# Constant rows of the stacked queries and keys: two batches in turn instead of four

## What is computed

```
# attention of layer 0, 16 heads of 8, S = 512
scores = (q @ k.T + c2p + p2c) / sqrt(8 * 3)
# c2p[i, j] = q[i] . pos_k[bucket(i - j) + 32], p2c[i, j] = k[j] . pos_k[32 - bucket(j - i)]
out = layernorm(softmax(scores) @ v @ Wo + bo + x)
# switch feed-forward, E = 8, F = 512
e = argmax(softmax(t @ switch_w + switch_b))
y = (gelu(t @ w1[e] + b1[e]) @ w2[e] + b2[e]) * max(route_prob)
```

## Time and profile before

| what | value |
|---|---|
| time of three runs | 761.99, 763.94, 764.26 us; median 763.94 us |
| span of the profiled execution (the page gives its span only, not the execution's whole time) | 759.0 us |
| busy share PE / DVE / ACT / POOL | 77% / 69% / 58% / 28% |
| moved by DMA | 130.80 MB, mean 172 GB/s |
| mean granted TensorE clock | 0.895 of full speed |

### The profile page before, as it was taken

How to read it: one execution, slowest core, us unless ns; L and a number is a source line. 1 busy time by engine, 2 the same in 40 slices (tenths; PEclk the granted TensorE clock), 3 DMA queues, 4 the chain that set the end, 5 groups by cost and what they waited for, 6 DMA issues and landing times. The chain is left out here.

```text
span 759.0 us, 16760 instructions
## 1 busy us (share of the span) xinstructions
PE 583.0 (77%) x5262; PEld 405.4 (53%) x5262; DVE 523.5 (69%) x1838; ACT 441.8 (58%) x960; POOL 209.7 (28%) x264
## 2 busy tenths in 40 slices
PE   4359967557999999999999999551997673578880
PEld 3258853234566565666666666441986342246550
DVE  7513235726778777899999997674224799867797
ACT  3225424336788788888888887560553443376723
POOL 1714424200950391059040000025344200211200
PEclk9999987877999999999999999755999697799885
DMA  9948834999999999999984540833553100000001
GB/s 245 258 149 292 260 104 129 282 320 324 267 363 325 233 278 332 313 223 273 323 242 114 137 110 2 252 74 108 175 188 108 30 1 0 0 1 1 0 1 56
DMA packets 130450, 130.80 MB, mean 172 GB/s; under 512 B 27148, under 2 KB 106876, under 8 KB 129468
## 3 DMA queue, kind: packets, MB, share of 16 engines
q1 hardware_dynamic: 121628, 101.88, 48.6%
q0 software_dynamic: 4032, 25.73, 9.1%
q10 hardware_dynamic: 4704, 2.11, 1.2%
HBM read 73.43 MB, written 52.92 MB: 166 GB/s over the span
## 5 line engine op out<-in xcount | busy, mean ns | idle before, releaser
L1526 DVE CUSTOM_DVE_ANT_0 l0am_prob<-l0am_ps_s,l0am_bias 128x512 f32<-128x512 f32 x256 | 161.6, 687 | 48.3 <-PE l0am_ps_s L1603 38.4
L1447 ACT ACTIVATE l0am_prob<-l0am_prob,l0am_neg_top 128x512 f32<-128x512 f32 x256 | 172.0, 729 | 11.9 <-DVE l0am_neg_top L1526 11.9
L1615 PE MATMUL l0am_ps_t<-c_ident,l0am_prob 128*128 128x128 f32 x1024 | 137.8, 278 | 0.0
L1615 PEld LDWEIGHTS l0am_ps_t<-c_ident,l0am_prob 128*128 128x128 f32 x1024 | 113.4, 142 | 16.8 <-issue 15.9
L613 ACT ACTIVATE l0f_h<-l0f_psU,l0f_experts 128x128 f32<-128x128 f32 x184 | 52.4, 368 | 84.2 <-PE l0f_psU L907 84.2
L1441 ACT COPY l0am_probT<-l0am_ps_t 128x512 f32<-128x512 f32 x128 | 69.0, 589 | 45.8 <-PE l0am_ps_t L1615 45.8
L1603 PE MATMUL l0am_ps_s<-l0am_ks,l0am_qs 32*128 32x512 f32 x512 | 73.9, 647 | 14.3 <-DVE l0am_neg_top L1526 11.1
L1513 DVE COPY l0am_probT<-l0am_ps_t 128x512 f32<-128x512 f32 x128 | 81.9, 681 | 2.3 <-PE l0am_ps_t L1615 2.1
L785 DVE COPY l0f_xsT<-l0f_psT 128x128 f32<-128x128 f32 x46 | 13.4, 291 | 90.9 <-PE l0f_psT L897 90.9
L1628 PE MATMUL l0am_ps_c<-l0am_probT,l0am_v 128*9 128x128 f32 x2048 | 67.9, 273 | 0.9 <-issue 0.9
L524 POOL DMA_INDIRECT token_results<-l0f_ys,l0f_token_i x46 | 44.2, 960 | 80.2 <-DVE l0f_ys L795 79.6
(11 more groups left out here) (319 smaller groups left out, 962.1 us busy)
## 6 DMA issues: line engine op xcount, KB each, us to landing
l0am_bias<-near_terms SPq DMA_DIRECT2D x128, 192.0 KB, 5.5
near_terms<-l0am_near POOLq DMA_DIRECT2D x6, 3072.0 KB, 13.0
l0f_mine<-l0f_experts SPq DMA_DIRECT2D x46, 256.0 KB, 2.6
near_terms<-l0am_near SPq DMA_DIRECT2D x2, 3072.0 KB, 10.9
l0am_rows_k<-position_k SPq DMA_DIRECT2D x12, 448.0 KB, 8.4
position_q<-l0am_rows SPq DMA_DIRECT2D x20, 224.0 KB, 5.3
position_k<-l0am_rows SPq DMA_DIRECT2D x20, 224.0 KB, 4.9
l0f_experts<-in_L_ffn_w SPq DMA_DIRECT2D x2, 2048.0 KB, 8.4
```

What stands on the lines that cost most here:

```text
L1447: nc.scalar.activation(prob[:, k, :], prob[:, k, :], ACT.Exp, bias=neg_top[:, k:k + 1], scale=-1.0)\
L1526: dve.tensor_tensor_reduce(out=prob[:, k, :], in0=ps_s[:, j, :], in1=bias[:, j, at:at + S], scale=-1.0, scalar=HUGE, op0=ALU.add, op1=ALU.min,
L1615: last = pe.transpose(ps_t[:, u % 2, i, :], prob[:, u % SLOTS_, i * P:(i + 1) * P], ident[:, :])
```

## The change

The stacks hold two batches (`STACKS = 2`); batch b uses place b % 2. So constant rows are stored for two batches only, four DMAs instead of eight. None is issued ahead of the slots; the four follow the loads of slots 2, 5, 8 and 11. Since batches 2 and 3 overwrite the places of batches 0 and 1, SP waits, ahead of the store of their q and k chunks, until the tiles of the last group of the batch b - 2 are loaded.

```diff
+STACKS = 2
...
-        "stack": [dram(f"stacked_{n}", (MARGIN + B * HEADS * 32 * FAR_PITCH,)) for n in "qk"],
+        "stack": [dram(f"stacked_{n}", (MARGIN + STACKS * HEADS * 32 * FAR_PITCH,)) for n in "qk"],
...
-        EARLY_BLOCKS, LATE_BLOCKS = 2, tuple(range(2, 20, 3))
+        LATE_BLOCKS = tuple(range(2, 2 + 3 * 2 * STACKS, 3))
...
                     aside.load(sp)
-                    for n in range(EARLY_BLOCKS):
-                        aside.store_blocks(sp, n)
...
                     if aside and s in LATE_BLOCKS:
-                        aside.store_blocks(sp, EARLY_BLOCKS + LATE_BLOCKS.index(s))
+                        aside.store_blocks(sp, LATE_BLOCKS.index(s))
...
-    BLOCK_STORES = 2 * B + 2
+    BLOCK_STORES = 2 * STACKS + 2
...
# store_chunk
-                        dst = bass.AP(dram["stack"][side].tensor, MARGIN + b * HEADS * 32 * FAR_PITCH,
+                        if b >= STACKS:
+                            last_group = GROUPS * (b - STACKS + 1) - 1
+                            sp.wait_ge(tiles_in[last_group % 2], 32 * (last_group // 2 + 1))
+                        dst = bass.AP(dram["stack"][side].tensor, MARGIN + b % STACKS * HEADS * 32 * FAR_PITCH,
...
# store_far
-                    dst = bass.AP(dram["stack"][side].tensor, MARGIN + (b * HEADS * 32 + first) * FAR_PITCH + col,
+                    dst = bass.AP(dram["stack"][side].tensor, MARGIN + (b % STACKS * HEADS * 32 + first) * FAR_PITCH + col,
...
# load_tiles
-                        src = bass.AP(dram["stack"][side].tensor, MARGIN + n * GROUP * 32 * FAR_PITCH, [(FAR_PITCH, P), (1, S)])
+                        src = bass.AP(dram["stack"][side].tensor, MARGIN + n % (STACKS * GROUPS) * GROUP * 32 * FAR_PITCH, [(FAR_PITCH, P), (1, S)])
```

## The result

The changed kernel takes 758.27 us, median of 11 runs (755.17 to 760.38). The kernel before, run again beside it, comes to 761.47 us over 11 runs (758.77 to 764.26), the three shown ahead among them. The ratio, with its 95% interval behind it, is 0.9943 [0.9925, 0.9961]: 4.3 us faster, between 3.0 and 5.7. The two medians lie 3.2 us apart; the interval holds both values. The gain is real and not far from the 5.5 us forecast, yet both of its terms were too big. So I read the profile by stretches.

The account below looks back on a forecast made before the run. Bound taken: chains through DMA at the router's end (POOL's issues, DMA, SP, PE) and at the last slots' token loads. Gains 3.0 + 2.5 = 5.5 us from 763.94 gave 758.4 us; range 755.8 to 761.6.

Parts of the forecast that it names:

- first term: Router's end: without the two early stores, SP's first load of tokens follows POOL's last scatter sooner, gaining 3.0 us.
- B: Rival, chance 0.10: no gain at the router's end, blank rows, scatters and loads of `mine` alone make the queue; 761.4 us.
- C: Rival, chance 0.11: no gain in the last slots, SP's pace sets them or the tail takes it back; 760.9 us.
- the second call is the nearest row: Step at the router's end: same POOL, ACT and SP instructions, so its 2.05 us distance was taken, gaining 3.0 us.
- small pieces: DMA at 35 to 41.5 us, first call: blank rows, scatters and loads of `mine`, engines busy at 209 GB/s.
- rule of turns packet by packet: Router's end: DMA engines alternate between queues per packet, so the last scatter wouldn't pay for the stores; gain near 0.
- second term: Last slots: without the stores behind slots 14 and 17, slots 18 to 22 take 8.24 us, not 10.78; gain 2.5.
- if the last tokens still take over 4: End of the slots: prediction wrong if last tokens are turned over 4 us after their load's issue; 4.90 before.
- SP's wait under 1 us: Attention, q chunk of batch 3: SP's added wait for group 7's tiles holds 0.6 us, covered by 3.9 us slack.
- rival D: Chance 0.06: slower, SP's wait for group 7's tiles at batch 3's q chunk delays bias loads; +4.1, 768.0 us.
- the same 644.2 us within 1: From the attention's first operation to the span's end: time unchanged; a deviation beyond 1 us makes the prediction wrong.
- as it is: Whole program: the runs' median is 4.94 us above the profiled span, taken as time around it and left unchanged.

Follow-up runs that it names:

- Each half alone: Changed kernel with the two late stores put back (only early ones gone): 0.996; with the two early stores put back (only late ones gone): 0.9964.

## Why the prediction was right, and where its terms were not

All profiles by what their layout has in common (us):

| what | with the stores | without | difference | forecast |
|---|---|---|---|---|
| end of last scatter to first load of tokens | 5.05, 5.53, 4.30, 5.12; mean 5.00 | 3.57, 3.39, 3.38, 3.41; mean 3.44 | 1.6 | 3.0 |
| turn of slot 18 to turn of slot 22 | 10.78, 9.89, 10.29, 9.75, 9.02; mean 9.95 | 8.79, 8.47, 8.09, 7.83, 8.13, 8.09; mean 8.23 | 1.7 | 2.5 |
| start of the attention (before; changed) | 114.81, 115.97, 114.21; mean 115.0 | 111.66, 111.47; mean 111.6 | 3.4 | 5.5 |

**The direction and both mechanisms were right.** Each half alone is still faster than before, with intervals that leave out 1, and each distance follows the stores ahead of it and no others. So the first term isn't absent, as B had it, nor the second, as C had it. (Left out of the first row are the kernels whose blank rows or loads of `mine` were moved; out of the second, the two whose slot loop holds no stores at all.)

**The first term was mis-sized, 1.6 us for 3.0.** The step that failed is "the second call is the nearest row, being the same instructions of POOL, ACT and SP". The instructions are the same, but not how the blank rows lie against the scatters: ACT issues its last transfer 1.7 us after POOL's last scatter in the changed kernel's first call (39.30 and 37.65), and 2.7 us after it in the second call of before (527.6 and 524.87). That this is the reason isn't shown, but with the last three held back the distance is 1.70, 1.82 and 2.02 us, so the missing 1.4 us were there to be had, by another edit; moving the loads of `mine` gave 0.9 of them in one profile. What I costed at nothing ("small pieces" at 35 to 41.5) was a third of the wait. Nor was the second call a fixed value: its distance is 1.81 to 2.82 us over nine profiles. Rival B had pointed at just these transfers; it went wrong in giving them all of it. Its rule of turns packet by packet would have made this term near 0; the distances decide against that, 5.00 with the stores and 3.44 without.

**The second term was mis-sized, 1.7 us for 2.5.** I took one execution's pair, 10.78 against 8.24. The lower end was right, 8.23 on average, but 10.78 is the longest of five with the stores. The last tokens took 3.41 and 3.89 us, where 2.5 was expected. My sign of being wrong, "if the last tokens still take over 4", was a bad one: they took 4.25 to 6.07 us in four profiles without the late stores. And over the whole loop the term is less sure than over the four slots, because of the 53.21 us with only the late stores gone; there the time, 0.9964 [0.9941, 0.9986], speaks for it, and the profile hardly does.

**The remaining steps.** Blank rows in 2 us: 2.2. A DMA share under a half at 31 to 35: 0.33. (That 4 us x 387 GB/s came to the stores' 1.57 MB was chance: in that window SP's queue moved 1.22 MB, the other queues the rest, and part of the stores had gone before.) SP's wait under 1 us: 0.3, and rival D fell, with the added waits alone at 0.9995. The scatters' own issue wasn't to move: the last one ended at 38.61 and 37.81, against 38.07. The slots were to take 49.9 us: 50.80 and 51.04, and the 53.21 told above, against 52.40, 52.84, 53.08 and 52.21 with the late stores. From the attention's start to the end, "the same 644.2 us within 1": 646.0 and 644.2, and 642.3 to 645.5 in the three profiles of the layout before. My bound of 1 us was narrower than the scatter of the same instructions, so by it the first profile alone would have called a right step wrong.

**The time was hit by two errors that cancel.** Against the profile I was 4.2 us short: span 757.7, forecast 753.5. In order of time: 1.7 at PE's first turn (43.93 for 42.2), 0.9 in the slots, 0.3 gained behind them, 1.8 behind the attention's start. And I left the 4.94 us between span and median "as it is". It isn't time around the span: in the repeated run of before it is 763.41 - 761.5 = 1.9 us, and in the changed kernel's 759.63 - 757.7 = 1.9. The other 3 us were scatter, a profiled execution that was short beside a median of three that lay 2.5 us above that of eleven. Base 761.47 less the local 3.4 is 758.1; measured, 758.27. In my sum, 763.94 less 5.5 came to 758.4: a base 2.5 us too high and a gain 2.1 us too big. That the time was hit within 0.2 us was luck.

## What to carry to other kernels

A second call of the same code is a good bound for a wait but not its value: compare also how the other engines' transfers lie against it, for what remains may hang on a neighbour that the change doesn't touch. Bulk stores off the path cost where small transfers close a chain, here the end of a scatter and the last loads of a loop, so look for the place where the DMA engines are idle and no chain runs through them; of the four places tried here none is free. Where terms are a few tenths of a per cent, take each distance from several profiles and the base from more than three runs, before a difference of one or two us is given a cause.

## What the runs showed of the hardware

- The engine that waits for the scatters went on 0.8 to 2.1 us after their last packet in nine profiles with blank rows of another engine's queue beside and behind them (2.1 in the changed kernel, of it 1.7 with no packet on any queue), and 0.7 to 0.8 us after it in the four where these were held back. In the second call of before it was 0.8 with blank rows behind it as well. In the first call the last blank rows landed 0 to 0.1 us ahead of SP's load in all six profiles that show it.
- Two stores whose bytes were through at 35 us (from there to 41.5 SP's queue moved 0.57 MB, without the stores 0.52) were followed by a DMA share of 1.02 until 41.5, where it is 0.54 without them (1.36 and 1.13 MB).
- The same store costs differently from execution to execution: the turns behind that of slot 5 lay 2.07, 2.53, 3.48, 3.69 and 5.10 us apart.
- The same last part of the program took 172.3 to 178.0 us over the profiles, the longest at a granted clock of 0.71 in its last stretch where before has 0.75.
